# Attention values in three rounded products, values projected last, and half of the output weights' low parts on GpSimd

## The reference

```python
q = (hidden_states @ Wq.T)...   # 32 query heads of 128, 8 key and value heads
k = (hidden_states @ Wk.T)...
v = (hidden_states @ Wv.T)...
q = q * cos + _rotate_half(q) * sin
k = k * cos + _rotate_half(k) * sin
scores = jnp.einsum('bgrqd,bgkd->bgrqk', qg, k) / jnp.sqrt(jnp.asarray(HD, q.dtype))
attn = jax.nn.softmax(scores.astype(jnp.float32), axis=-1).astype(q.dtype)
out = jnp.einsum('bgrqk,bgkd->bgrqd', attn, v)
return out @ Wo.T
```

## Time and profile before

| | |
|---|---|
| median of 3 runs | 3009.76 us (3008.11 to 3013.42) |
| the profiled execution | 3008.69 us, span 3007.0 us |
| TensorE busy | 2797.8 us, 93% of the span |
| VectorE busy | 1781.2 us, 59% |
| ScalarE busy | 985.2 us, 33% |
| GpSimd busy | 129.9 us, 4% |
| mean granted TensorE clock | 0.966 of full speed |
| stretch 300 to 2440 us (the attention stage) | TensorE busy 2083.30 us, VectorE 1319.69, ScalarE 699.94, GpSimd 0.00, granted clock 0.99 |

### The profile page before, as it was taken

How to read it: one execution, slowest core, us unless ns; L and a number is a source line. 1 busy time by engine, 2 the same in 40 slices (tenths; PEclk the granted TensorE clock), 3 DMA queues, 4 the chain that set the end, 5 groups by cost and what they waited for, 6 DMA issues and landing times. The chain is left out here.

```text
span 3007.0 us, 37373 instructions
## 1 busy us (share of the span) xinstructions
PE 2797.8 (93%) x13193; PEld 2280.7 (76%) x13193; DVE 1781.2 (59%) x3197; ACT 985.2 (33%) x2026; POOL 129.9 (4%) x76
## 2 busy tenths in 40 slices
PE   7994899999899999989999998999999888749999
PEld 6772688888788888877888887888888766548888
DVE  4887565566665555667665566766556556563322
ACT  3453333333333323333333234333323324431110
POOL 2110000000000000000000000000000000241100
PEclk9996899999999999999999999999999998979999
DMA  5320322223222222312222221222222111010000
GB/s 111 77 57 0 113 75 78 76 73 98 63 92 77 77 77 77 98 61 81 91 77 77 77 83 57 96 94 77 77 77 77 56 57 42 1 71 22 29 28 29
DMA packets 55468, 207.19 MB, mean 69 GB/s; under 512 B 6784, under 2 KB 7168, under 8 KB 53312
## 3 DMA queue, kind: packets, MB, share of 16 engines
q1 hardware_dynamic: 55360, 205.79, 21.5%
HBM read 197.37 MB, written 8.39 MB: 68 GB/s over the span
## 5 line engine op out<-in xcount | busy, mean ns | idle before, releaser
L987 PE MATMUL at_proj<-qr_xhi,at_whi 128*128 128x512 f32 x1536 | 628.5, 409 | 13.2 <-DVE at_wlo L869 8.8
L989 PE MATMUL at_proj<-qr_xhi,at_wlo 128*128 128x512 f32 x1536 | 602.5, 392 | 0.0
L988 PE MATMUL at_proj<-qr_xlo,at_whi 128*128 128x512 f32 x1536 | 601.1, 391 | 0.0
L987 PEld LDWEIGHTS at_proj<-qr_xhi,at_whi 128*128 128x128 f32 x1536 | 290.2, 189 | 77.0 <-DVE at_wlo L869 9.4
L988 PEld LDWEIGHTS at_proj<-qr_xlo,at_whi 128*128 128x128 f32 x1536 | 290.5, 189 | 63.5 <-issue 7.5
L989 PEld LDWEIGHTS at_proj<-qr_xhi,at_wlo 128*128 128x128 f32 x1536 | 289.5, 188 | 63.7
L1032 PE MATMUL at_out<-at_wohi,at_ohi 128*128 128x512 f32 x1008 | 312.2, 391 | 6.2 <-DVE at_wolo L874 4.2
L1032 PE MATMUL at_out<-at_wohi,at_olo 128*128 128x512 f32 x1008 | 311.3, 390 | 0.0
L1032 PE MATMUL at_out<-at_wolo,at_ohi 128*128 128x512 f32 x1008 | 311.2, 390 | 0.0
L744 ACT COPY at_pT<-at_tp 128x512 f32<-128x512 f32 x128 | 75.2, 588 | 598.5 <-PE at_tp L1008 598.5
L865 DVE TENSOR_TENSOR at_olo<-at_ov,at_ohi 128x512 fp32r<-128x512 f32 x128 | 88.5, 692 | 307.0 <-ACT at_ohi L749 307.0
(11 more groups left out here) (238 smaller groups left out, 4215.9 us busy)
## 6 DMA issues: line engine op xcount, KB each, us to landing
at_wstage<-in_w_qkv_dram SPq DMA_DIRECT2D x192, 512.0 KB, 3.6
at_ostage<-in_w_o_dram SPq DMA_DIRECT2D x128, 512.0 KB, 4.5
cv_x<-in_x_dram SPq DMA_DIRECT2D x32, 512.0 KB, 6.7
out_dram<-h SPq DMA_DIRECT2D x16, 512.0 KB, 2.6
fn_w_lo_raw<-in_w_t_dram SPq DMA_DIRECT2D x8, 512.0 KB, 7.1
fn_qka_lo_raw<-in_qka_t_dram SPq DMA_DIRECT2D x5, 512.0 KB, 5.8
sc_fhi_raw<-in_dft_fwd_dram SPq DMA_DIRECT2D x4, 512.0 KB, 7.8
sc_chi_raw<-in_lag_cos_dram SPq DMA_DIRECT2D x2, 512.0 KB, 9.9
```

Source lines behind the costliest of these rows:

```text
L987: pe.matmul(proj[:, j % 2, :], hi[:, w], x_hi[:, k, :], start=(k == 0), stop=False)
L988: pe.matmul(proj[:, j % 2, :], hi[:, w], x_lo[:, k, :], start=False, stop=False)
L989: last = pe.matmul(proj[:, j % 2, :], lo[:, w], x_hi[:, k, :], start=False, stop=(k == KT - 1))
```

## The change

Three edits, all in the attention stage.

1. `values` becomes three rounded products. The transposed values and probabilities get a high part from the ScalarE copy that was there already (`v_rows`, `pT_out`, which now write F32R tiles) and a low part from a new VectorE subtraction each: `v_low` once a pass, `p_low` for each batch. Both read PSUM and one SBUF tile. TensorE waits for `p_low` where it waited for `pT_out`, and for `v_low` where it waited for `v_rows`.
2. The values tile is projected as tile 5 instead of tile 1 (`TILE_AT`). `v_out` moves to the end of ScalarE's list, the queries' `rope_out` each move one tile ahead. `vT` now shares its memory with `pT_hi`.
3. `low_o` of heads 2 and 3 goes from VectorE to GpSimd, with a semaphore of its own.

Beside that some lines of the lists move: on ScalarE `o_split(n)` goes ahead of `pT_out(n+1)`, on VectorE `top_of(n+1)` goes ahead of the keys' `rope_out`, and `o_split` ahead of `top_of`.

```diff
+TILE_AT = (0, 2, 3, 4, 5, 1)
+VALUES = TILES - 1
...
-                    act.copy(pT[:, :], tp[:, :]).then_inc(pT_done, 1)
+                    act.copy(pT_hi[:, :], tp[:, :]).then_inc(phi_done, 1)
...
+            @block.gpsimd
+            def _(pool):
+                def step(qt, g, par, att, nxt, turn):
+                    if att:
+                        s = head_at(qt, g)
+                        for r in (2, 3):
+                            after(pool, wohi_done, s * HEADS + r + 1)
+                            pool.tensor_tensor(wo_lo[:, r, :], o_stage[r % 2][:, :], wo_hi[:, r, :].bitcast(F32),
+                                               ALU.subtract).then_inc(wolo_done[1], 1)
+                steps(pool, lambda: None, step)
...
+                def v_low(s):
+                    after(dve, vhi_done, s + 1)
+                    dve.tensor_tensor(v_lo[:, :, :], tp[:, :].rearrange("p (b d) -> p b d", d=D),
+                                      v_hi[:, :, :].bitcast(F32), ALU.subtract).then_inc(vlo_done, 1)
+
+                def p_low(n):
+                    after(dve, phi_done, n + 1)
+                    dve.tensor_tensor(pT_lo[:, :], tp[:, :], pT_hi[:, :].bitcast(F32), ALU.subtract)\
+                       .then_inc(plo_done, 1)
...
-                def values(n, par, b):
-                    after(pe, pT_done, n + 1)
+                def values(n, b):
+                    after(pe, plo_done, n + 1)
                     after(pe, olo_done, n)
-                    pe.matmul(ov[:, :], v[par][:, b, :], pT[:, :], start=True, stop=True).then_inc(ov_mm, 1)
+                    pe.matmul(ov[:, :], v_hi[:, b, :], pT_hi[:, :], start=True, stop=False)
+                    pe.matmul(ov[:, :], v_lo[:, b, :], pT_hi[:, :], start=False, stop=False)
+                    pe.matmul(ov[:, :], v_hi[:, b, :], pT_lo[:, :], start=False, stop=True).then_inc(ov_mm, 1)
```

More of the change, by code:

```diff
@@ L587, in attention_stage @@
         kT = [sb(f"at_k{i}", [P, QT]) for i in range(2)]
-        vT = sb("at_vT", [P, QT])
-        v = [sb(f"at_v{i}", [P, QB, D]) for i in range(2)]
+        v_hi, v_lo = (sb(f"at_v{n}", [P, QB, D], F32R) for n in ("hi", "lo"))
         probs = sb("at_probs", [P, HEADS, P])
-        pT = sb("at_pT", [P, HEADS * P])
+        vT, pT_hi = landing(nc, ctx, "at_pThi", [P, HEADS * P])
+        pT_lo = sb("at_pTlo", [P, HEADS * P], F32R)
         o_hi = sb("at_ohi", [P, HEADS * P], F32R)
@@ L608, in attention_stage @@
         whi_done, wlo_done = sem("at_whi_done"), sem("at_wlo_done")
-        wohi_done, wolo_done = sem("at_wohi_done"), sem("at_wolo_done")
+        wohi_done, wolo_done = sem("at_wohi_done"), [sem(f"at_wolo_done{i}") for i in range(2)]
         ahead = sem("at_ahead")
@@ L708, in step @@
                             if ahead == 0 or nxt:
-                                after(sp, wolo_done, s * HEADS + what[1] + 1)
+                                after(sp, wolo_done[what[1] // 2], s * 2 + what[1] % 2 + 1)
                                 load_o(s + ahead, g + ahead, r)
@@ L893, in step @@
                     stats = turn_next or for_next_stage
+                    if att:
+                        v_low(s)
                     if turn:
@@ L910, in step @@
                         low_o(s, 1)
+                        if not turn:
+                            top_of(n + 1, 1)
                     if nxt:
@@ L913, in step @@
                     if att and not turn:
-                        top_of(n + 1, 1)
+                        p_low(n)
                     if nxt:
@@ L919, in step @@
                             normalize(n + 1)
+                        o_split(n)
                         top_of(n + 2, 2)
-                        o_split(n)
-                        low_o(s, 2)
-                        low_o(s, 3)
+                    if nxt:
+                        rope_out(s + 1, 1 - par, 1)
+                    if att:
+                        if not turn:
+                            p_low(n + 1)
                         normalize(n + 2)
@@ L928, in step @@
                     if att:
+                        o_split(n + 1)
                         top_of(n + 3, 3)
-                        o_split(n + 1)
+                        p_low(n + 2)
                         add(qt, n, 0, nxt)
@@ L942, in step @@
                         o_split(n + 2)
+                        p_low(n + 3)
                         add(qt, n + 1, 1, nxt)
@@ L978, in project @@
                         after(pe, rows.lo_done, (qt + 1) * rows.UNITS)
[L980 to L981 removed]
+                    if j == 1:
+                        after(pe, vT_done, s)
                     else:
[L983 removed]
+                        after(pe, roped, s * ROPED + (0 if j == 0 else j - 1))
                     hi, lo = w_hi[j % 2], w_lo[j % 2]
```

58 lines of the change are left out of this document (28 added, 30 removed).

## The result

| | before | change |
|---|---|---|
| median | 3010.97 us (3008.11 to 3013.42, 4 runs) | 3036.15 us (3034.0 to 3038.54, 4 runs) |
| span of the profiled execution | 3007.0 us | 3036.8 us |
| mean granted TensorE clock | 0.966 | 0.964 |

The ratio is 1.0084 [1.0067, 1.0102]: the change is 25 us slower. The prediction said 3043 us, slower. The sign, the place and the main mechanism were right. Edits 1 and 2 gained 14 us more than forecast, GpSimd's subtractions cost 6 us more than forecast, and the two misses partly cancel.

What follows compares the result with a forecast made beforehand. TensorE, busy 93% of the span, was taken as the bound. Terms -21.6 + 53.2 - 2 + 4 = +33.6 us on the profiled 3008.7 gave 3042.3, 3043 us against the median; range 2991 to 3072.

Steps and rivals of the forecast that it cites:

- Edit 1 on TensorE, -21.6 us: Values products in attention: three rounded products replace one float32 product, saving 0.17 us in each of 128 batches, 21.6 us.
- Edit 1 on VectorE, 0: Plain pass: VectorE's five added subtractions just fit, with 0.14 us margin before TensorE's second-batch transposes, so no cost.
- the rival that VectorE itself becomes the bound, 3004 us: Plain passes: the 0.14 us margin is wrong and p_low comes 0.5 us late in each; 3004 us, chance 8%.
- Edit 3, 28 stalls of 1.9 us = 53.2: Plain passes: GpSimd's head 2 subtraction holds up VectorE's second normalization, so TensorE stalls 1.9 us in each of 28.
- the point that decides: Plain pass: the normalization's start at 20.46; GpSimd released before it (forecast about 19.8) blocks it, after it does not.
- The rival of a late GpSimd, 2993 us: Plain passes: GpSimd starts behind the normalization, costing only 0 to 0.2 us a pass; 2993 us, chance 20%.
- The rival of the clock: Behind the stalls TensorE runs at half clock in half or more passes, adding 24 to 48 us; 3067 to 3091, 15%.
- Edit 2, -2 us: Values tile last: the pass without attention loses a 2.5 us wait for a 0.6 us copy, once; other passes gain nothing.
- The other passes, +4 us: The three turns and the last pass: each 0 to 2.4 us longer, taken as 1 us each, 4 us.
- The sum: All terms together: +33.6 us on the profiled 3008.7 us, given as 3043 us against the median.

Runs made afterwards that it cites:

- Run 4: The kernel before with values as three identical rounded products of the high parts, no VectorE work for low parts added: 2988.33 us, ratio 0.993.
- run 1: The change with low_o of heads 2 and 3 back on VectorE instead of GpSimd: 2971.18 us, ratio 0.9876 to before.
- run 2: The change with one more wait: GpSimd starts head 2's subtraction only when the second batch's normalization is done: 2975.76 us, ratio 0.989.
- run 3: The kernel before with only low_o of heads 2 and 3 moved to GpSimd: 3010.39 us, ratio 1.0004.
- run 5: The change with GpSimd's subtraction for head 2 made twice in every pass: 3033.11 us, ratio 1.0085.
- run 6: The change with each GpSimd subtraction split into two instructions of 512 columns: 2997.99 us, ratio 0.9968.
- run 7: The kernel before with only the values tile projected last, its copy v_out and the queries' rotations moved accordingly: 2992.06 us, ratio 0.9947.

## Why the prediction was right, and where it was wrong

**Edit 1 on TensorE, -21.6 us: right.** Run 4 has -21.0. Three rounded products are 0.227 us apart in the change too (1289.88, 1290.11, 1290.33). The 131 ns that the prediction quoted from the Trainium skill, "TensorE: Matmul & The Clock Gate", section "Back-to-back issue gap", and turned down, do not hold for these products: the measurement decides.

**Edit 1 on VectorE, 0: right.** Edits 1 and 2 together (run 1) give -38.1 us, edit 1's products alone -21.0 and edit 2 alone -15.8, together -36.8. Nothing measurable is left for the five new subtractions. With it falls the rival that VectorE itself becomes the bound, 3004 us.

**Edit 3, 28 stalls of 1.9 us = 53.2: right in kind and size.** Measured are 1.94 in the pass shown. Over the 24 ordinary plain passes the change is 1.93 us a pass longer than run 1 (the rest of the difference from first to last `turn_v`, 2069.31 against 2001.68, when the turns and the passes named below are taken out). The stall is in 27 of the 28 passes, 25 times through the normalization and twice through `at_wlo`. Runs 1, 2, 3, 5 and 6 show the mechanism from five sides: without GpSimd no stall, with GpSimd later none, with edit 3 alone none, with more GpSimd work the same, with shorter instructions half of it.

**The rival of a late GpSimd, 2993 us: it did not happen**, but one pass shows what it would have been like. In the pass behind the first turn GpSimd's subtractions ran as a pair from 901.47, later than the normalization, and that pass took 63.19 us, the length of run 1. In the pass shown first the release was 0.7 us ahead of the point that decides: GpSimd at 1290.01, the normalization at 1290.70. The prediction had 0.66. That the two agree is in part luck. The prediction held the release to come in the same rhythm in pass after pass, but where the normalization was blocked GpSimd started anywhere from 0.16 to 1.34 us ahead of it. The forecast was safe because only the late side was open: a release that is earlier still meets `at_wlo` instead, at the same price.

**The rival of the clock: it happened in few passes.** In the twentieth, TensorE waits 1.88 us and then goes at half clock from 1639.77 to 1643.18. TensorE's starts, then the windows (length, busy by engine, granted clock, DMA share, GB/s) of that stretch:

```profile
1638.36 0.66 PE L1044 MATMUL at_tp<-ident,at_probs 128*128 128x128 f32 x4 [1.88 <-DVE at_probs L876]
...
1640.62 0.63 PE L1023 MATMUL at_proj<-qr_xhi,at_whi 128*128 128x512 f32 x1
1641.05 0.63 PE L1024 MATMUL at_proj<-qr_xlo,at_whi 128*128 128x512 f32 x1
```

```profile
1640.00:1642.00 2.00, 2.00 (x6) 1.51 (x6) 1.90 (x4) 2.00 (x10) 1.34 (x1) 0.50 0.39 150
```

Products are 0.43 us apart there, and the pass takes 66.83 us instead of 65.1. The same happens in the first pass, behind a wait of 1.96 us (67.28 us, where run 1 has 63.69), and in the pass behind the second turn, where the granted clock is 0.50 from 1441.80 to 1445.20, behind a wait of 2.02 us (68.95 us against 65.91 in run 1). Beyond the stalls these three passes are 4.4 us longer than in run 1, not the 24 to 48 of the rival.

**Edit 2, -2 us: wrong, it is -15.8.** The step that failed is "In all other passes the copy of the values hides behind the last `outputs` [...]: nothing". It held for the plain passes. For the turns the prediction asked what the moved step's new place is covered by, and never what had stood behind it in its old place, the statistics of the next quarter. And in the first pass the wait of 2.5 us was priced without the half clock behind it, although show just that behind 1.96 us.

**The other passes, +4 us: wrong, in both directions.** The last pass became 3.0 us shorter instead of 1 longer. Its waits for `at_olo` fell from 1.89 + 1.96 + 1.47 us to 1.03 + 1.47; run 1 has the short last pass too (52.22 us) and run 7 has not (55.84), so it comes with edit 1's list, in which the split of the output (`at_ohi`, `at_olo`) stands ahead of the maximum. Which of its moves does it was not tried alone. The turns with GpSimd are 11.0 us longer together than in run 1 (240.3 against 229.3), against 3 forecast. The trace splits them: 6.4 us are busy time of the same list at a lower granted clock, 4.6 are standing. Of the standing 4.3 are two collisions of the same kind as in the plain passes, with `at_wlo`. VectorE in the first turn, then TensorE in the first and in the second:

```profile
835.92 3.37 DVE L896 TENSOR_TENSOR at_wlo<-at_wstage,at_whi 128x1024 fp32r<-128x1024 f32 x1
...
839.35 0.50 PE L1023 MATMUL at_proj<-qr_xhi,at_whi 128*128 128x512 f32 x1 [2.14 <-DVE at_wlo L896]
...
1374.25 0.49 PE L1023 MATMUL at_proj<-qr_xhi,at_whi 128*128 128x512 f32 x1 [2.15 <-DVE at_wlo L896]
```

So the collision in the turns is 4.3 us, close to the forecast of 3. Whether the lower clock there is a consequence of GpSimd stays open. Against it: run 5, with more work on GpSimd, has less busy time in its turns (210.6 us), and run 6 less still (209.5).

**The sum.** Edits 1 and 2 bring 38.1 us (run 1 against before); forecast were 23.6. Putting the subtractions on GpSimd costs 63.3 us more (25.2 + 38.1, each taken against the runs of before beside it); forecast were 53.2 + 4. So +25 and not +34: the forecast was 14 us too low on one side and 6 too low on the other. That the total came within 8 us is luck in part, since the two misses have opposite signs. The direction did not hang on it, as the stall alone is larger than both gains together.

## What to carry to other kernels

Moving an instruction to an idle engine doesn't make it free: if the GpSimd instruction and one of VectorE both read two SBUF tiles (and run 2 shows one with a single SBUF input held up as well), look at the moment at which the moved instruction is released, and at what stands next on the other engine. Here one semaphore wait (run 2) turned 25 us slower into 34 us faster, and not moving the work at all (run 1) was best, because in a plain pass VectorE was not what TensorE waited for. When a step is moved away, price its old place as well: what stood behind it on that engine now comes earlier. In this kernel the edit was worth 16 us, in the first pass, the turns and the passes behind them, which the prediction had not followed.

## What was not expected of the hardware

- The half clock does not go by the length of the wait before it alone. Waits of 1.88 and 1.96 us were followed by half clock some 1.4 us after TensorE had resumed, one of 2.02 us (at 1441.21) by half clock 0.6 us after, while another wait of 1.88 us (at 1228.27) and one of 2.00 us (at 1032.74) in the same execution, with the same work behind them, were not. What tells them apart was not found.
- The collision is not told by who is named in a wait. In a plain pass TensorE's waits name VectorE's normalization, and GpSimd's part shows only in durations: 2.63 us for 0.69, 3.38 for 1.23, 2.77 for 2.39. An instruction's row includes the time for which the other engine keeps it out, so a group's mean that has grown while its size has not (1077 ns against 691) is what to look for.
